# One lane instead of two in the scan of a delta-rule layer

## What is computed

```python
S0 = jnp.zeros((BH, DK, DV), x.dtype)          # BH = 2 * 16 heads, DK = DV = 16
def step(S, inp):
    qt, kt, vt, at, bt = inp
    v_hat = jnp.einsum('bij,bi->bj', S, kt)
    err = vt - v_hat
    S = at[:, None, None] * S + bt[:, None, None] * (kt[:, :, None] * err[:, None, :])
    o = jnp.einsum('bij,bi->bj', S, qt)
    return (S, o)
_, O = lax.scan(step, S0, (Q, Kh, V, alpha, beta))   # over 2048 tokens
```

## Time and profile before

| | us |
|---|---|
| median of 3 runs | 4886.96 |
| lowest and highest | 4878.78, 4890.54 |
| the profiled execution | 4886.68 |
| span of its profile, first to last instruction | 4884.9 |
| busy: PE, DVE, ACT, POOL | 3811.3, 3865.6, 3062.1, 1846.0 |

### The profile page before, as it was taken

One profiled execution on the slowest core, in us unless ns is written; L12 is line 12 of the kernel. 1 busy time (PEld: TensorE's weight loads), 2 busy tenths in 40 slices (PEclk: granted clock), 3 DMA queues, 4 the chain that ended last, 5 costly groups with the idle time before them and its releaser, 6 DMA issues. The chain is left out here.

```text
span 4884.9 us, 64394 instructions
## 1 busy us (share of the span) xinstructions
PE 3811.3 (78%) x16142; PEld 1479.4 (30%) x16142; DVE 3865.6 (79%) x5725; ACT 3062.1 (63%) x4245; POOL 1846.0 (38%) x1828
## 2 busy tenths in 40 slices
PE   7986002656556896987589999999999999999468
PEld 3432001545443342342122222222222222222123
DVE  5536697999994663368789999999999999998352
ACT  5568101222222563337469999999999999999242
POOL 1000683666661101106424444444444444444112
PEclk9999555777778998989889999999999999999789
DMA  1013545444442000024511111111011111110300
GB/s 45 9 48 87 72 88 117 102 89 100 97 93 73 11 7 11 0 81 155 169 30 31 34 38 38 38 37 38 23 37 37 38 38 38 37 22 5 112 10 35
DMA packets 126458, 265.24 MB, mean 54 GB/s; under 512 B 41296, under 2 KB 70864, under 8 KB 117904
## 3 DMA queue, kind: packets, MB, share of 16 engines
q1 hardware_dynamic: 124208, 252.56, 21.6%
q10 hardware_dynamic: 1952, 9.18, 0.6%
HBM read 170.26 MB, written 91.26 MB: 54 GB/s over the span
## 5 line engine op out<-in xcount | busy, mean ns | idle before, releaser
L1032 POOL TENSOR_TENSOR att_heads_rest<-att_heads_probs,att_heads_high 128x352 f16<-128x352 f32 x1024 | 873.5, 853 | 1242.3 <-DVE att_heads_rest L1184 1182.6
L1164 DVE TENSOR_REDUCE att_heads_maxima<-att_heads_peek 128x1 f32<-128x1024 f32 x992 | 1209.1, 1219 | 42.3 <-PE att_heads_peek L1059 42.3
L1132 ACT ACTIVATE att_heads_probs<-att_heads_scores 128x1024 f32<-128x1024 f32 x1024 | 1057.8, 1033 | 171.2 <-PE att_heads_scores L1078 153.7
L1078 PE MATMUL att_heads_scores<-att_heads_q,att_heads_k 128*128 128x512 f16 (+1 forms) x4096 | 1075.2, 385 | 32.1 <-issue 28.8
L1134 ACT ACTIVATE att_heads_high<-att_heads_scores 128x1024 f16<-128x1024 f32 x1024 | 1054.5, 1030 | 0.0
L1184 DVE TENSOR_TENSOR att_heads_rest<-att_heads_probs,att_heads_high 128x672 f16<-128x672 f32 x1024 | 882.9, 862 | 69.1 <-POOL att_heads_rest L1032 55.4
L1903 PE MATMUL delta_scan_sums<-delta_scan_o_terms,main_identity 128*128 128x256 f32 x1536 | 412.7, 437 | 604.4 <-POOL delta_scan_o_terms L1971 604.4
L1059 PE MATMUL att_heads_peek<-att_heads_k,att_heads_q 112*128 112x512 f16 x1984 | 599.9, 383 | 18.2 <-DVE att_heads_maxima L1164 17.1
L1903 PEld LDWEIGHTS delta_scan_sums<-delta_scan_o_terms,main_identity 128*128 128x128 f32 x1536 | 340.9, 224 | 676.5 <-POOL delta_scan_o_terms L1971 617.6
L1078 PEld LDWEIGHTS att_heads_scores<-att_heads_q,att_heads_k 128*128 128x128 f16 (+1 forms) x4096 | 319.2, 98 | 708.1 <-issue 461.2
L1094 PE MATMUL att_heads_out<-att_heads_high,att_heads_v_head 128*64 128x512 f16 x2048 | 418.6, 405 | 15.3 <-DVE att_heads_rest L1184 14.7
(11 more groups left out here) (247 smaller groups left out, 4677.0 us busy)
## 6 DMA issues: line engine op xcount, KB each, us to landing
delta_scan_record<-delta_record SPq DMA_DIRECT2D x64, 898.0 KB, 9.4
att_heads_q<-att_hel SPq DMA_DIRECT2D x192, 128.0 KB, 3.1
att_heads_k<-att_hel SPq DMA_DIRECT2D x192, 128.0 KB, 3.2
att_hel<-att_hel_high SPq DMA_DIRECT2D x32, 512.0 KB, 4.4
att_hel<-att_hel_rest SPq DMA_DIRECT2D x32, 512.0 KB, 5.0
delta_record<-delta_chunks_record SPq DMA_DIRECT2D x64, 224.5 KB, 4.3
att_o<-att_heads_out_copy SPq DMA_DIRECT2D x256, 32.0 KB
att_out_parts<-att_o ACTq DMA_DIRECT2D x8, 1024.0 KB, 15.7
```

The source lines that it names most:

```text
L1032: nc.gpsimd.tensor_tensor(rest[:, step % 4, SPLIT:], probs[:, step % 4, SPLIT:], high[:, step % 4, SPLIT:], ALU.subtract).then_inc(rest_b_ ...
L1078: mm = nc.tensor.matmul(scores[:, step % 2, tokens(j)], k[0:rows, slot, number, tile * P:(tile + 1) * P], q[0:rows, slot, number, tokens(h ...
L1132: nc.scalar.activation(probs[:, step % 4], scores[:, step % 2], ACT.Exp, scale=LOGIT_SCALE).then_inc(probs_ready, 1)
L1164: nc.vector.tensor_reduce(maxima[:, m:m + 1], peek[:].rearrange("p j n -> p (j n)"), AX.X, ALU.max).then_inc(peek_read, 1)
```

## The change

One number: the four value columns of a partition are no longer divided.

```diff
     C = CHUNK
-    LANES = 2
+    LANES = 1
     JL = JQ // LANES
     COLUMNS = CHUNKS * JQ * C
```

## The result

The changed kernel takes 4960.14 us (median of 4 runs, 4954.92 to 4965.77) against 4888.75 us for the kernel before (4 runs). The ratio is 1.014 with a 95% interval of 1.0126 to 1.0154: slower, 7 us above the forecast of 4953 us and inside its range.

A forecast was written before the change was run, and what follows sets the result against it. VectorE's order of work in the scan was taken as the bound. Durations of 2851 ns plus four 34 ns gaps give 2987 against 2730 ns a chunk, 66 us more: 4886.7 + 66 = 4953 us, range 4940 to 4981 us.

The forecast's parts named there:

- What bounds: In the scan, VectorE's own order of work sets the time: busy 699.06 of 699.07 us, 2.730 us a chunk.
- The gap: In the scan, each of a chunk's four instructions starts 34 ns after the end of the one ahead.
- The durations: Wide scan instructions: two products of 687 ns, reductions of 722 and 755 ns, together 2851 ns a chunk.
- the bounds named for them: Signs for the scan's reductions: 715 to 725 ns with 544 elements, 749 to 758 ns with 576.
- rows 7: Profile rows of instructions begun after a wait, operands in SBUF: product of 768 elements 954 ns, reductions 955 and 1755 ns.
- The sum: Scan chunk of 2987 ns against 2730 ns, 66 us over 256 chunks; whole kernel 4953 us, 1.4% slower.
- What was costed at nothing: ScalarE's copies, GpSimd's products, record loads, loop turns, the single memset and later stages were taken to add no time.
- ScalarE's decayed state: ScalarE's scaled state copy, done 1.16 us into a chunk; the last reduction could begin at 2.20 us, so no wait.
- The loop's turn: Scan loop's turn, once in 16 chunks, hidden behind a 755 ns reduction; if it showed, fifteen turns would be 2 us.
- a change in their length: Stages after the scan should only start later; the prediction is wrong if they change their length.
- The first rival: Waits in the scan cost nothing: 2.482 us a chunk, 64 us less in all, 4823 us; chance 5%.
- The second rival: Last reduction, with two waits, starts after 0.14 us: 0.10 us a chunk, 26 us more, 4979 us; chance 7%.

The follow-up runs named there:

- both tiles in SBUF: The change with state and error in SBUF in place of PSUM: 5191.67 us, ratio 1.062.
- uneven lanes: The kernel before with two lanes of three columns and one column in place of two and two: 4888.56 us, ratio 1.000.
- two chains in PSUM: The change with even and odd chunks as two alternating independent recurrences, which changes the result, state and error in PSUM: 4834.98 us, ratio 0.9887 to the kernel before.

## Why the prediction was right

- *What bounds.* VectorE's own order in the scan, with nothing else near. The scan grew by 69 us, the medians lie 71 us apart.
- *The gap.* 34 ns was taken from two other stages; 35.5 us over 1024 instructions is 35 ns. That the wait was for a register's value made no difference.
- *The durations.* Products: 687 ns forecast, 686 and 687 measured. Reductions: 722 and 755 forecast, 728 and 760 measured, just above the bounds named for them. This term was mis-sized: rows 7 are reductions that write SBUF, and writing PSUM after a wait costs 7 to 8 ns more, as the run with both tiles in SBUF shows. The prediction had put "a few ns longer on PSUM" into the range, not into the sum.
- *The sum.* 686 + 728 + 687 + 760 + 4 x 35 = 3001 ns against 2987: 3 us over the kernel. The forecast was 66 us for the scan; it came to 69. Of the 7 us by which the whole lies above the forecast 3 are these, 2 are the kernel before (4888.75 against the 4886.7 us that the sum started from), and 2 are the rest. That the rest is so small is partly luck: the last mixture alone was 8 us longer in both profiles of the change, and small differences elsewhere took most of that back.
- *What was costed at nothing.* ScalarE's decayed state was done 1.1 us ahead (a cover of one microsecond had been worked out). The loop's turn showed no gap: the starts of successive chunks lie at most 3.02 us apart. What was not true is that later stages stay as they are to the microsecond: a change in their length was one of the prediction's signs of being wrong, and the last mixture showed it (below).
- *The first rival.* That waits cost nothing fell by its own test: starts lie 35 ns behind the ends, where it needed 30 ns ahead. Its price was right, however: the run with wide instructions and no wait on the one ahead gained 61 us in the scan (699.07 against 638.16 us) where 64 were worked out. Counting instructions gave the right answer there, where no instruction reads the one ahead of it.
- *The second rival.* No longer gap stands ahead of the last reduction: 1105.83 + 0.69 = 1106.52, then 1106.55.

All these kinds fall into one sum. The bare work of a chunk, wide and without a wait, is 2.49 us. Two lanes add four instructions of 61 ns: 2.73 us. One lane adds four waits of 126 ns (0.72 against 0.595 us for a product): 3.00 us. Four lanes add twelve instructions of 61 ns: 3.22 us, which is what was measured inside the loop.

## What to carry to other kernels

Where each instruction on VectorE reads what the one ahead wrote, work out both prices from the trace before merging: one more instruction costs its start-to-start time less its elements (61 ns here), a wait on the one ahead about twice that (126 ns: it starts 35 ns behind the end in place of 80 to 90 ns before it). So at these sizes splitting a chain into two interleaved halves pays and four parts do not. The halves need not be equal: parts of three columns and one were as fast as two and two.

## What the runs showed of the hardware that was not expected

**Two SBUF inputs beside GpSimd.** With state and error in SBUF, a product of 512 elements took 693 ns at the least and up to 1711 ns. The timelines of VectorE and of GpSimd in that run:

```profile
1103.89 1.71 DVE L1978 TENSOR_TENSOR delta_scan_s_terms<-delta_scan_record,delta_scan_error 128x512 f32<-128x512 f32 x1
```

```profile
1103.79 1.27 POOL L1966 TENSOR_TENSOR delta_scan_o_terms<-delta_scan_state_copy,delta_scan_record 128x512 f32<-128x512 f32 x1 [1.23 <-ACT delta_scan_state_copy L1931]
```

GpSimd's product had begun 0.10 us ahead and ended at 1105.06, 1.17 us into VectorE's, which was 1.02 us longer than the shortest. VectorE's ended 1105.60 - 1105.06 = 0.54 us behind GpSimd's, and so did all others: in the 511 products of this run that began more than 0.15 us before the end of a running product of GpSimd, the end came 0.53 to 0.54 us behind that end, however long they had been under way by then. With one input in PSUM, as in the change, the same second product beside the same work of GpSimd took 686 to 691 ns, though GpSimd was busy through all of each. The Trainium skill, "SBUF — State Buffer", section "SBUF: two separate sides", says that of a VectorE instruction with two SBUF inputs and a GpSimd instruction that reads SBUF, the one that starts first has a shared pair of ports for the whole instruction and the other is blocked. The trace agrees in the main: the end is tied to GpSimd's end, but by 0.54 and not the 0.69 us of a whole product. That keeping state and error in PSUM avoids it is shown by the runs.

**The clock of an untouched stage.** The windows view of the last mixture, first in the kernel before, then in the change:

```profile
4681.80:4884.90 203.10, 158.58 (x624) 54.76 (x624) 60.80 (x180) 61.05 (x95) 41.76 (x35) 0.89 0.07 27
```

```profile
4752.30:4964.00 211.70, 168.04 (x624) 56.49 (x624) 60.80 (x180) 61.25 (x95) 41.75 (x35) 0.84 0.07 26
```

The same 624 matmuls keep TensorE busy for 9.5 us more, and the granted clock, a mean over its two levels (2.4 and 1.2 GHz), is 0.84 in place of 0.89 of full speed. Most of it comes from one stretch: some 45 us into the stage the clock goes to the lower level, for 20 us in the kernel before and for 34 us in the change. The second profiles show the same pair of numbers. With uneven lanes, whose scan is as long as that of before, the last mixture ran at 0.89 and the first, the same stage 2.8 ms earlier, at 0.84 (0.87 in the kernel before). In the other five runs, whose scan is longer or shorter than that of before, the last mixture took 208.8 to 211.0 us at 0.85 or 0.86; the run that is faster than the kernel before, with two chains in PSUM, is among them with 210.6 us. So the clock of a stage that a change does not touch can move by some 8 us of run time, whether the change gains or loses; that it is the shift of the stage in time fits, but what decides it stays open.

**The loop's turn.** A loop of 256 VectorE instructions lost 2.4 us on average at each turn, with instructions fetched again each time, one of 128 nothing that shows in the chunk's mean. Where between the two this begins was not tried.
